# Spreading the late routing of a mixture-of-experts stage over four groups, and closing the last group in halves

## What is computed

```python
scores = sigmoid(xf @ gate_w.T)
_, sel = top_k(scores + expert_bias, 2)
# for each chosen expert e, weight s = scores[token, e]:
h   = silu((s * x) @ w1[e].T) * ((s * x) @ w3[e].T)
out = shared(x) + sum over the two experts of s * (h @ w2[e].T)
x   = layernorm(x + out)
```

## Time and profile before

| what | value |
|---|---|
| median of the runs | 787.43 us |
| the profiled execution, its own time | 788.83 us |
| its span | 786.7 us |
| busy over the span | TensorE matmul 750.0 us, VectorE 645.2, ScalarE 512.5, GpSimd 479.0 |
| groups 2 and 3 begin | 481.25 and 504.84 us |
| step 8 of group 15 begins | 772.17 us |
| last matmul, last store issued, end of span | 778.50, 783.98, 786.7 us |

### The profile page before, as it was taken

How to read it: one execution, slowest core, us unless ns; L and a number is a source line. 1 busy time by engine, 2 the same in 40 slices (tenths; PEclk the granted TensorE clock), 3 DMA queues, 4 the chain that set the end, 5 groups by cost and what they waited for, 6 DMA issues and landing times.

```text
span 786.7 us, 20507 instructions
## 1 busy us (share of the span) xinstructions
PE 750.0 (95%) x6948; PEld 525.1 (67%) x6948; DVE 645.2 (82%) x1386; ACT 512.5 (65%) x1037; POOL 479.0 (61%) x653
## 2 busy tenths in 40 slices
PE   2889999999999999999999999899999999999995
PEld 1345555555555555555554688788888888888885
DVE  7689899999999999999998547976776666666665
ACT  1158788888888888888889645445545444554542
POOL 4345587876767667676634465565565566555554
PEclk9999999999999999999999999999999999999998
DMA  4646766566656665565531654454555545565440
GB/s 116 174 116 165 213 175 182 147 164 178 153 158 163 173 170 154 157 162 166 151 82 36 180 127 106 104 144 123 130 124 129 129 129 127 124 131 124 121 97 27
DMA packets 201449, 108.84 MB, mean 138 GB/s; under 512 B 10392, under 2 KB 200984, under 8 KB 201368
## 3 DMA queue, kind: packets, MB, share of 16 engines
q1 hardware_dynamic: 200048, 105.88, 52.1%
q10 hardware_dynamic: 1320, 1.91, 1.1%
HBM read 73.41 MB, written 33.82 MB: 136 GB/s over the span
## 4 chain that ended last, share of the span: by engine, by line
PE 86%; DVE 6%; DMA 3%; issue 2%; SPq 2%; ACT 1%; POOL 0%; POOLq 0%; DVEq 0%; ACTq 0%
PE bank L879 15%; PE bank L714 15%; PE bank L686 10%; PE bank L721 8%; PE bank L722 8%; PE bank L723 8%; PE bank L699 7%; PE bank L790 2%; PE bank L770 2%; PE bank L810 2%; DVE negmax L1014 2%; PE bank L777 2%; PE bank L794 2%; PE bank L817 1%; DMA q_stack<-max_rows 1%
## 5 line engine op out<-in xcount | busy, mean ns | idle before, releaser
L1014 DVE TENSOR_REDUCE negmax<-bank 128x2 f32<-128x512 f32 x512 | 320.1, 679 | 15.2 <-PE bank L699 12.8
L561 ACT ACTIVATE probs<-bank 128x512 f32<-128x512 f32 x512 | 291.8, 606 | 60.8 <-PE bank L686 57.0
L665 ACT ACTIVATE q_stack<-k_stack 128x512 f32<-128x512 f32 x128 | 80.8, 631 | 154.9 <-DVE k_stack L1077 154.9
L699 PE MATMUL bank<-k_stack,q_stack 48*128 48x256 bf16 x1024 | 162.7, 282 | 13.9 <-DMA k_stack<-k_parts_dram 9.8
L686 PE MATMUL bank<-q_stack,k_stack 50*128 50x256 bf16 x1024 | 156.2, 274 | 4.2 <-DMA q_stack<-max_rows 2.1
L1077 DVE TENSOR_TENSOR k_stack<-bank,probs 128x512 f32<-128x512 f32 x128 | 88.3, 690 | 74.8 <-PE bank L723 74.4
L714 PE MATMUL bank<-probs,v_aug 128*32 128x256 f32 x2048 | 137.1, 385 | 0.4 <-ACT attT L572 0.4
L686 PEld LDWEIGHTS bank<-q_stack,k_stack 50*128 50x128 bf16 x1024 | 75.2, 95 | 87.6 <-ACT probs L561 44.4
L721 PE MATMUL bank<-x_hi,hi_w 128*128 128x512 f32 x288 | 126.5, 439 | 3.1 <-DVE k_stack L1087 1.2
L722 PE MATMUL bank<-x_hi,lo_w 128*128 128x512 f32 x288 | 114.0, 396 | 0.0
L723 PE MATMUL bank<-x_lo,hi_w 128*128 128x512 f32 x288 | 113.6, 394 | 0.0
(11 more groups left out here) (103 smaller groups left out, 1111.3 us busy)
## 6 DMA issues: line engine op xcount, KB each, us to landing
probs<-route_dram SPq DMA_DIRECT2D x128, 256.0 KB, 4.9
q_stack<-q_parts_dram SPq DMA_DIRECT2D x64, 192.0 KB, 3.3
k_stack<-k_parts_dram SPq DMA_DIRECT2D x64, 192.0 KB, 4.1
k_parts_dram<-k_parts SPq DMA_DIRECT2D x32, 192.0 KB, 2.2
q_parts_dram<-q_parts SPq DMA_DIRECT2D x32, 192.0 KB, 2.1
xT_sb<-xT SPq DMA_DIRECT2D x32, 128.0 KB, 2.3
k_parts_dram<-k_parts SPq DMA_DIRECT2D x32, 128.0 KB, 2.0
q_parts_dram<-q_parts SPq DMA_DIRECT2D x32, 128.0 KB, 1.9
```

Of the source, the lines that this page charges most:

```text
L561: nc.scalar.activation(probs[h][:], score_ps[EXP_BANK[h]][:].rearrange("p (j t) -> p j t", j=NT), ACT.Exp).then_inc(exp_done, 1)
L665: nc.scalar.activation(act[n % DEPTH], gated[n % DEPTH] if n else up1_ps[0][:], ACT.Silu).then_inc(act_set, 1)
L699: mm = pe.matmul(max_ps[MAX_BANK[h]][:, i * T:(i + 1) * T], q_stack[b.ring][first:last, h // 2, i * P:(i + 1) * P], k_stack[b.ring][first: ...
L1014: nc.vector.tensor_reduce(negmax[b.ring % 2][:, :, column], max_ps[MAX_BANK[h]][:].rearrange("p (i s) -> p i s", i=NT), AX_X, ALU.max, neg ...
```

## The change

Two things that have nothing to do with each other.

The late routing is spread over more steps. The exponential stands behind step 1 of group 2; the sixteen instructions stand in steps 3, 5, 7 and 8 of groups 2 and 3 and steps 3 and 5 of group 4; the turn, the copy and the store stand in group 5, where they stood in group 3. Groups 0 to 5 are written out, and the loop takes 4 iterations where it took 5.

The end of the last group is rearranged. The scaled product of its step 8 is made by VectorE, not GpSimd. Within group 15 the residual and statistics of group 14 stand in step 3 (before: 6), mean and variance in step 5 (before: 7), and the power before step 6's product on GpSimd (before: behind step 8). Group 15's down products go to two banks, tiles 0 and 1 to one and tiles 2 and 3 to the other, which is the bank of group 14; so the first of them waits for group 14's residual sum. The closing work is done for tiles 0 and 1, which are announced when their part of the last down product is done, and then for tiles 2 and 3, with buffers of its own; SyncE stores the first half and ScalarE's queue the second. The normalising of group 14 stands behind the scaled product and ahead of both halves.

```diff
-        LATE_ROUTING = 2
+        LATE_FIRST, LATE_LAST = 2, 5
+        WRITTEN = LATE_LAST + 1
...
-            for g in range(4):
+            for g in range(WRITTEN):
                 body(g, g % 2)
-            with engine.Fori(0, (GROUPS - 6) // 2) as i:
...
+            with engine.Fori(0, (GROUPS - WRITTEN - 2) // 2) as i:
...
@@ SyncE
-            write_out(GROUPS)
-            sp.wait_ge(y_out, 16 * GROUPS)
+            sp.wait_ge(last_y_set, GT // 2)
+            sp.dma_start(out[N // P - GT:N // P, :, :].rearrange("i p c -> p i c")[:, HALVES[0]], last_y[:, HALVES[0]]).then_inc(y_out, 16)
+            sp.wait_ge(y_out, 16 * GROUPS + 16)
@@ GpSimd
+                    if last and n == LAST_POW_AT:
+                        pool.wait_ge(eps2_set, g)
+                        pool.tensor_tensor(rstd2[:], var_eps2[:], minus_half[:], ALU.pow).then_inc(rstd2_set, 1)
-                    if n:
+                    if n and not (last and n == NE - 1):
...
-            pool.wait_ge(eps2_set, GROUPS)
-            pool.tensor_tensor(rstd2[:], var_eps2[:], minus_half[:], ALU.pow).then_inc(rstd2_set, 1)
+            for half, tiles in enumerate(HALVES):
+                pool.wait_ge(last_eps_set, half + 1)
+                pool.tensor_tensor(last_rstd[:, tiles], last_eps[:, tiles], minus_half[:, tiles], ALU.pow).then_inc(last_rstd_set, 1)
@@ ScalarE
-                    if isinstance(g, int) and (g, n) == (LATE_ROUTING, 0):
...
+                    if isinstance(g, int) and (g, n) == (LATE_FIRST, 1):
+                        act_e.wait_ge(logits_set, B)
+                        nc.scalar.activation(scores[:, EARLY:TILES, :], logits[:, EARLY:TILES, :], ACT.Exp, scale=-1.0).then_inc(exp_logits, 1)
...
+            act_e.wait_ge(last_y_set, GT)
+            act_e.dma_start(out[N // P - GT:N // P, :, :].rearrange("i p c -> p i c")[:, HALVES[1]], last_y[:, HALVES[1]]).then_inc(y_out, 16)
@@ TensorE, down
+                if closing and n == 0:
+                    pe.wait_ge(res2_set, GROUPS - 1)
+                if last:
+                    pe.wait_ge(last_scaled, 1)
...
+                firsts = (0, GT // 2) if closing else (0,)
                 for i in range(GT):
-                    mm = pe.matmul(down_ps[r][:, i * P:(i + 1) * P], (hid_s if n else hid)[n % DEPTH][:, i * P:(i + 1) * P], w2_sb[:, n, :],
-                                   start=(n == 0 and i == 0), stop=(n == NE - 1 and i == GT - 1))
+                    if last and i == GT // 2:
+                        mm.then_inc(last_tokens, 1)
+                    mm = pe.matmul(down_ps[r if not closing or i < GT // 2 else 1 - r][:, i * P:(i + 1) * P], (hid_s if n else hid)[n % DEPTH][:, i * P:(i + 1) * P], w2_sb[:, n, :],
+                                   start=(n == 0 and i in firsts), stop=(n == NE - 1 and i + 1 in firsts[1:] + (GT,)))
@@ VectorE
+            def late_routing(g, n):
+                a, b = EARLY, TILES
+                if (g, n) == (LATE_FIRST, 3):
                     dve.wait_ge(exp_logits, 2)
+                    sigmoid(a, b)
+                if (g, n) == (LATE_FIRST, 5):
+                    with_bias(a, b)
+                if (g, n) in ((LATE_FIRST, 7), (LATE_FIRST + 1, 7)):
+                    highest(a, b)
+                if (g, n) in ((LATE_FIRST, 8), (LATE_FIRST + 1, 8)):
+                    by_rank(a, b)
+                if (g, n) == (LATE_FIRST + 1, 3):
+                    first_of_ranked(a, b, first_sel)
+                if (g, n) == (LATE_FIRST + 1, 5):
+                    without_first(a, b)
+                if (g, n) == (LATE_FIRST + 2, 3):
+                    first_of_ranked(a, b, equal)
+                if (g, n) == (LATE_FIRST + 2, 5):
+                    weights_of_both(a, b)
...
+            dve.wait_ge(hid_set, done(GROUPS - 1, NE - 1))
+            dve.wait_ge(square_set, GROUPS * E)
+            dve.wait_ge(down_mm, done(GROUPS - 1, NE - 1 - DEPTH))
+            nc.vector.tensor_tensor(hid_s[(NE - 1) % DEPTH], hid[(NE - 1) % DEPTH], weight2_b[E - 1], ALU.mult).then_inc(last_scaled, 1)
             norm(GROUPS - 1)
-            stats_of(GROUPS, 1)
-            dve.wait_ge(stats2_set, GROUPS * GT)
-            aggregate(GROUPS)
-            norm(GROUPS)
+            for half, tiles in enumerate(HALVES):
+                last_rows(half, tiles)
+            for half, tiles in enumerate(HALVES):
+                dve.wait_ge(last_rstd_set, half + 1)
+                for i in range(tiles.start, tiles.stop):
+                    nc.vector.tensor_scalar(last_y[:, i, :], last_res[:, i, :], last_mv[:, i, 0:1], last_rstd[:, i:i + 1],
+                                            ALU.subtract, ALU.mult).then_inc(last_y_set, 1)
```

More of the change, by code:

```diff
@@ L393, in group @@
                         write_out(g - 2)
-                if isinstance(g, int) and g == LATE_ROUTING + 1:
+                if isinstance(g, int) and g == LATE_LAST:
                     route_to_dram(slice(CHUNKS - 1, CHUNKS), 2)
@@ L506, in group @@
             def group(g, r):
+                last = isinstance(g, int) and g == GROUPS - 1
                 for n in range(NE):
-                    if n:
+                    if last and n == LAST_POW_AT:
+                        pool.wait_ge(eps2_set, g)
+                        pool.tensor_tensor(rstd2[:], var_eps2[:], minus_half[:], ALU.pow).then_inc(rstd2_set, 1)
+                    if n and not (last and n == NE - 1):
                         if past(g, 1) or n > DEPTH:
@@ L523, in group @@
                         keep_transposed(TAILS[1])
-                    if n == POW_AT and past(g, 1):
+                    if n == POW_AT and past(g, 1) and not last:
                         pool.wait_ge(eps2_set, g)
@@ L872, in down @@
                     pe.wait_ge(logits_set, B)
-                if n % NE:
+                closing = isinstance(g, int) and g * NE + n >= (GROUPS - 1) * NE
+                last = isinstance(g, int) and g * NE + n == GROUPS * NE - 1
+                if closing and n == 0:
+                    pe.wait_ge(res2_set, GROUPS - 1)
+                if last:
+                    pe.wait_ge(last_scaled, 1)
+                elif n % NE:
                     pe.wait_ge(hids_set, routed(g, n))
@@ L956, in first_of_ranked, with sigmoid @@
                 route(nc.vector.tensor_tensor(sel[:, tiles], equal[:, tiles], best[:, tiles].unsqueeze(2).to_broadcast(full), ALU.is_equal))
-            def biased_scores(a, b):
+            def sigmoid(a, b):
                 tiles = slice(a, b)
@@ L1122, in delayed @@
                     hidden(g, m)
-            def late_routing(n):
-                if n == 1:
+            def late_routing(g, n):
+                a, b = EARLY, TILES
+                if (g, n) == (LATE_FIRST, 3):
                     dve.wait_ge(exp_logits, 2)
[L1127 to L1139, removed]
+                    sigmoid(a, b)
+                if (g, n) == (LATE_FIRST, 5):
+                    with_bias(a, b)
+                if (g, n) in ((LATE_FIRST, 7), (LATE_FIRST + 1, 7)):
+                    highest(a, b)
+                if (g, n) in ((LATE_FIRST, 8), (LATE_FIRST + 1, 8)):
+                    by_rank(a, b)
+                if (g, n) == (LATE_FIRST + 1, 3):
[6 more added lines that the diff above has]
+                    weights_of_both(a, b)
             def group(g, r):
+                last = isinstance(g, int) and g == GROUPS - 1
+                mean_at, stats_at = (LAST_MEAN_AT, LAST_STATS_AT) if last else (MEAN_AT, STATS_AT)
                 for n in range(NE):
-                    if n == MEAN_AT and past(g, 1):
+                    if n == mean_at and past(g, 1):
                         dve.wait_ge(stats2_set, g * GT)
```

56 lines of the change are left out of this document (42 added, 14 removed).

## The result

The changed kernel's median is 781.43 us (six runs, 780.35 to 782.25) against 787.56 for the kernel before beside it (six runs, 786.7 to 788.23). The ratio is 0.9913, 95% interval 0.9890 to 0.9936, which is 780.6 us (778.8 to 782.4) from 787.43. The direction is as forecast. The two medians themselves stand as 0.9922 to 1, which would be 781.3, inside the range; in eight more runs the same kernel had a median of 782.03 and a ratio of 0.9931 (0.9903 to 0.9959). So part of the difference is scatter, and part is not. The rest of this text tells the two apart.

The account below looks back on a forecast made before the run. TensorE was taken to bound the kernel (86% of the chain), with 3.55 us waiting on VectorE and 8.2 us after its last matmul. Routing 3.5 plus end 1.8 is 5.3; 787.43 - 5.3 = 782.1 us, range 781.1 to 784.4.

Parts of the forecast that it names:

- The routing: Part one: TensorE's waiting for VectorE in groups 2 and 3 goes when the late routing is spread; 3.5 us taken.
- the thinnest place: Step 5 with the statistics behind the routing: `hidden` 6 ends at 774.05, needed at 774.47; 0.4 us left, no stall.
- the turned routing (L737) is 0.30 of it and stays: Of the 3.85 us lost between group 2 and step 2 of group 3, the turn's 0.30 was held not recoverable.
- the margin from 3.55 to 3.5: Part one's waiting was put at 3.55 us if nothing is left; the forecast took 3.5.
- The end up to the store: Last group, part two: the last store is issued 1.73 us earlier; with its landing, 1.8 taken.
- so I give it 0.1: Landing of the last store, 128 KB and not 256 KB: 0.1 us gained, from a row where 128 KB took 2.1.
- the 3.3 of the row with that queue: A store on ScalarE's queue landed in 3.3 us, 1.2 later; as the low bound it makes part two's gain 0.6.
- I cost both at nothing: Six written groups and the wait for the routing's store between groups 5 and 6 were both put at zero cost.
- The upper bound of both gains: Both parts at their best, 3.55 + 2.2: 781.7 us, less half a microsecond for the median's scatter, 781.1.
- A residual stall: Rival: a comparison falls behind a GpSimd product at steps 5 to 8, routing gains 2.0; 783.6 us, chance 0.14.
- The queue and bank of the end: Rival: late landing on ScalarE's queue or a wait at group 14's bank; gain 4.1, 783.3 us, chance 0.10.
- The slower case: Rival: routing instructions push each `hidden` on in-order VectorE; 793.5 us unabsorbed, slower once stalls pass 5.35; chance 0.03.

## Why the prediction came out as it did

**The routing: right in mechanism, 0.24 us short.** No step of groups 2 to 5 waits for VectorE. The layout from the pattern of a full group held closely. Counted from the start of step 8:

| what | laid out | measured |
|---|---|---|
| end of the comparison of step 7 | 2.60 | 2.64 (501.82 - 499.18) |
| end of `hidden` 7 | 3.93 | 3.97 |
| end of `hidden` 6 in group 4, the thinnest place | 1.88 | 1.83 |

The timeline of VectorE that the first two rest on (L975 is L949 of before, L1119 and L1129 are `weigh` and `hidden`), and GpSimd's product beside it:

```profile
500.50 1.32 DVE L975 TENSOR_TENSOR q_stack<-q_stack,best 128x128 f32<-128x128 f32 x1
501.86 0.69 DVE L1119 TENSOR_TENSOR k_stack<-bank,probs 128x512 f32<-128x512 f32 x1
502.47 0.68 DVE L1129 TENSOR_TENSOR k_stack<-bank,q_stack 128x512 f32<-128x512 f32 x1
```

```profile
500.41 1.27 POOL L529 TENSOR_TENSOR k_stack<-q_stack,probs 128x512 f32<-128x512 f32 x1 [1.70 <-ACT probs L665]
```

In all, three of the sixteen instructions stood behind GpSimd for about 1.05 us (1.32, 1.32, 1.38), and six did before.

The step that failed in this part is "the turned routing (L737) is 0.30 of it and stays"; it makes 0.19 of the 0.24, and the rest is the margin from 3.55 to 3.5. The step with the turn takes only 0.10 more here, in each of the profiles with the spread, and 0.31 or 0.32 in each with the old routing. I took the instruction's duration for its cost. In the kernel before, the last routing instruction ended at 509.25 and the turn began at 509.40; the weight load before it shows that TensorE had been idle:

```profile
509.37 0.14 PEld L737 LDWEIGHTS bank<-ident,q_stack 128*128 128x128 f32 x1 [0.41 <-issue]
```

The profile puts the 0.41 down to issue. I read it as the last piece of the waiting for VectorE: it went away with the rest in every profile with the spread, and stayed in every one without.

**The end up to the store: right.** 1.80 us earlier by the stages, 1.73 in the working. VectorE's scaled product stood behind GpSimd's and ended at 772.43, 4.44 after step 8 began (laid out: 4.4). TensorE still had the products before it to do, and the last matmul ended 0.2 sooner. The bank that group 15 shares cost no wait. The power out of the way of the residual was 1.0 of it, as the variant with the early norm shows.

**The landing: 0.4 us short, the largest miss in the span.** The step that failed is "so I give it 0.1"; the stage gave 0.52. I gave a store of half the size 0.1, from a row of attention transfers at 2.1 us that ran beside others. At the end of the kernel it landed in 1.8, and on ScalarE's queue too; the 3.3 of the row with that queue, which made the low bound of the gain, did not recur here. Of the 0.52 us, 0.34 is the size, as the variant with one store shows. The rest, 2.72 against 2.54 for 256 KB, I have not settled.

**The written groups: put at nothing, 0.35 us.** The prediction says of the six written groups and of the store's new place "I cost both at nothing". In the stages that holds. But its last step took the gain of the span off the median of the times, as if the part outside the span stayed, and that part fell by 0.35 us in every kernel with six groups written out, also in the one with nothing else changed.

**The range.** With the right terms the sum is 3.74 + 1.80 + 0.52 + 0.35 = 6.4, and the forecast would have been 781.0, already a tenth below the low end of the range. The upper bound of both gains had no room for the turn (3.55 at most), and none for the part outside the span. The remaining 0.4 to the ratio's 780.6 is within the scatter of the runs: the medians' own quotient gives 781.3, and later runs of the same kernel gave 0.9931. The low end took half a microsecond for that scatter, from three runs; between single executions the begin of group 0 moves by up to 6.4.

**The rivals.** A residual stall did not occur. The queue and bank of the end cost nothing. The slower case had its place right (VectorE's queue in order, GpSimd in the way) and its point far off: it took six further comparisons at two places to lose 2.8 us, about half of the 5.35 that would decide.

## What to carry to other kernels

Small work on a busy in-order engine should go where the engine it feeds has slack, one piece for each step, and not beside other work of the same step. Slack read from one steady period of the timeline (when the product is done, when the next reader asks) predicted the three placements that I compared to 0.05 us, and the slack of one to 0.1. When a wait is taken away, look for its last piece under another name: an instruction that starts just after the late engine's last one is late too. At the end of a kernel, what has no reader until then (a power, a norm) should be done before the last product, and the last store should be small. Where the start of a kernel scatters by microseconds, compare stages, not spans. And compare the time with the span too: what lies outside the span can change with the code.

## What the runs showed of the hardware

Normalising from SBUF to SBUF on VectorE, one tensor input and two scalars for each partition, stands behind GpSimd too: four took 2.74 us beside GpSimd's products and 1.10 alone. I had expected this only of instructions with two SBUF inputs. The Trainium skill (SBUF — State Buffer, Who interferes with whom) names `tensor_scalar` among the operations that can take the port that both share; this trace agrees. The variant with the early norm has the same picture, with 2.73 us.

An 8 KB transfer that TensorE's next step needs held it up for 3.15 us in one execution (below, the timeline of TensorE in the variant with GpSimd's product), and not at all at this place in nine of the 13 profiles, all with the same attention. Of that variant's ten timed runs, three took 786.4 to 787.3 us and seven 781.1 to 781.9; the profiled one was of the three, and whether the two others had the same cause is not shown. Behind this wait, and behind those of 3.2 and 1.8 us in the two other late profiles, the granted clock was at its lower level for some microseconds; behind the 1.6 us of the kernel before it was not. Why the transfer is late now and then, no run here shows.

```profile
97.04 0.39 PE L703 MATMUL bank<-q_stack,k_stack 50*128 50x256 bf16 x1 [3.15 <-DMA q_stack<-max_rows]
```
